# A recurrent mixer with a small expert layer on one core: batch 5's up products move between the last projections, and the up weights' rows are centred

## The reference

```python
shifted = pad(hidden)[:, :-1]
key, value, rec = (hidden * m + shifted * (1 - m) for m in (mix_k, mix_v, mix_r))
k = key @ Wk;  v = value @ Wv;  r = sigmoid(rec @ Wr)
rwkv = _wkv(time_decay, time_first, k, v)     # a recurrence over the 512 tokens
x = layernorm(hidden + (r * rwkv) @ Wo)
...
gate = softmax(x @ router_w.T) * top2_mask     # 8 experts of width 16
h = einsum('bth,eih->beti', x, down_w);  a = silu(h)
out = layernorm(x + sum_e gate_e * (a_e @ up_w_e))
```

## Time and profile before

| | |
|---|---|
| median of 3 runs | 495.65 us (495.41 to 495.65) |
| profiled execution | 495.26 us |
| its span, first to last instruction | 493.4 us |
| TensorE busy | 471.9 us, 96% |
| VectorE busy | 408.8 us, 83% |
| ScalarE busy | 338.7 us, 69% |
| GpSimd busy | 259.5 us, 53% |
| TensorE's granted clock | 0.986 of full speed over the span |

### The profile page before, as it was taken

The page is one execution under the profiler, slowest core; times in us unless marked ns, Lnnn a source line. Parts: engine busy times, 40 slices in busy tenths (PEclk is TensorE's granted clock), DMA queues, the critical chain, the costliest instruction groups (busy, mean ns, idle before and its releaser), DMA issues. The chain is left out here.

```text
span 493.4 us, 6302 instructions
## 1 busy us (share of the span) xinstructions
PE 471.9 (96%) x1850; PEld 316.4 (64%) x1850; DVE 408.8 (83%) x655; ACT 338.7 (69%) x769; POOL 259.5 (53%) x279
## 2 busy tenths in 40 slices
PE   8998799999999999999999999999999999999991
PEld 3444377777777667775777667776677656776550
DVE  6998988897799878997799977998699977776686
ACT  1568365865867678786777769776787767657574
POOL 2446764566515964457625767259635574321326
PEclk9999799999999999999999999999999999999997
DMA  9800250003000042004110032001320012300015
GB/s 248 277 12 1 86 191 1 0 3 85 1 1 0 24 147 87 1 1 129 64 64 1 1 129 106 22 1 63 107 89 1 0 43 86 128 1 1 1 38 219
DMA packets 20098, 30.35 MB, mean 62 GB/s; under 512 B 2016, under 2 KB 7136, under 8 KB 20064
## 3 DMA queue, kind: packets, MB, share of 16 engines
q1 hardware_dynamic: 20064, 29.95, 18.6%
HBM read 21.56 MB, written 8.39 MB: 61 GB/s over the span
## 5 line engine op out<-in xcount | busy, mean ns | idle before, releaser
L514 ACT ACTIVATE PR<-PR 128x512 f32<-128x512 f32 x128 | 74.3, 581 | 53.0 <-PE PR L296 23.1
L320 PE MATMUL PP<-WO,RW 128*128 128x512 f32 x216 | 97.3, 592 | 0.0
L1026 POOL TENSOR_SCALAR NM<-SUM,RS 128x1 f32<-128x1 f32 x30 | 9.1, 302 | 157.3 <-ACT RS L514 157.3
L320 PEld LDWEIGHTS PP<-WO,RW 128*128 128x128 f32 x216 | 39.5, 190 | 41.3 <-issue 40.9
L1020 POOL TENSOR_TENSOR DQ<-DEN,EX 128x512 f32<-128x512 f32 x32 | 41.0, 1282 | 35.4 <-DVE DEN L730 35.4
L767 DVE TENSOR_TENSOR RW<-NU,PR 128x512 f32<-128x512 f32 x32 | 22.0, 687 | 42.3 <-ACT PR L514 42.2
L778 DVE SCALAR_TENSOR_TENSOR KT<-D,VEC,XT 128x512 f32<-128x512 f32 x56 | 52.0, 959 | 0.0
L292 PE MATMUL PV<-VH,WVH 128*128 128x512 f32 x112 | 47.0, 420 | 0.4 <-DVE NU L754 0.4
L292 PE MATMUL PK<-KH,WKH 128*128 128x512 f32 x112 | 47.2, 422 | 0.0
L730 DVE TENSOR_TENSOR_SCAN DEN<-PK,EX 128x512 f32<-128x512 f32 x32 | 39.1, 1221 | 9.7 <-ACT EX L514 7.5
L292 PE MATMUL PR<-RH,WRH 128*128 128x512 f32 x112 | 47.0, 419 | 0.2 <-DVE RW L767 0.2
(11 more groups left out here) (200 smaller groups left out, 1119.2 us busy)
## 6 DMA issues: line engine op xcount, KB each, us to landing
XT<-in_xt SPq DMA_DIRECT2D x32, 256.0 KB, 3.6
XN<-in_x SPq DMA_DIRECT2D x28, 256.0 KB, 2.7
out<-XN SPq DMA_DIRECT2D x28, 256.0 KB, 2.0
WO<-in_wo SPq DMA_DIRECT2D x1, 1024.0 KB, 7.7
XT<-in_x SPq DMA_DIRECT2D x4, 256.0 KB, 4.1
out<-XT SPq DMA_DIRECT2D x4, 256.0 KB, 2.2
X1T<-in_wk SPq DMA_DIRECT2D x2, 256.0 KB, 4.9
XN<-in_wv SPq DMA_DIRECT2D x2, 256.0 KB, 5.3
```

Source lines behind the costliest of these rows:

```text
L320: last = eng.matmul(projected_at(t), RW[(C * b + c) % NRW][:, 128 * n:128 * n + 128], WO[:, c, :], start=(c == 0), stop=(c == C - 1))
L514: eng.activation(*a, **k).then_inc(q[s], 1)
L1026: eng.tensor_scalar(NM1[:, col(t)], total, RS1[:, col(t)], scale, ALU.mult, ALU.mult)\
```

## The change

Three things change, and the queues are rewritten around them.

Order of the up products: in slots 12 to 28 `ffn_up(t3 + 3)` goes behind the projection. In the tail the transposes of batch 6 (`ffn_turn(LAST - 1)`) come ahead of the last projection, into bank PP, and their copy goes to the buffer NU instead of AGT; batch 5's four up products stand between the last projection, the transposes and the hidden products of batch 7.

Centring: the rows of UP (each row belongs to one expert's hidden unit and has 512 outputs) lose their mean once, in slot 4. The tile that the up product is added to is normalised and has mean zero, so the sum has mean zero too. The second norm then needs no mean: the square has no offset, the addition gives no sum, NM falls away, and a normalisation is one multiplication with RS.

Bookkeeping: MEASURED has three tiles (29, 30, 31) instead of five and FINISHED one (31) instead of two; tiles 24 and 25, and 26 and 27, share one logarithm and one exponential (`spread2(t, 2)`).

```diff
-        MEASURED = [NT * (LAST - 2) + 3, NT * (LAST - 1) + 1, NT * (LAST - 1) + 3, NT * LAST + 1, NT * LAST + 3]
+        MEASURED = [NT * LAST + 1, NT * LAST + 2, NT * LAST + 3]
-        FINISHED = [NT * LAST + 1, NT * LAST + 3]
+        FINISHED = [NT * LAST + 3]
...
-                self.agt = (DQ if tail else AGT)[:, 128 * lo:128 * hi]
-                self.turned_at = ((PK[0], PH)[lo // 2] if tail else PK[1] if k == LAST - 1 else PU)[:, 0:128 * (hi - lo)]
+                self.agt = (DQ if tail else NU if k == LAST - 1 else AGT)[:, 128 * lo:128 * hi]
+                self.turned_at = ((PK[0], PH)[lo // 2] if tail else PP if k == LAST - 1 else PU)[:, 0:128 * (hi - lo)]
...
-                if j == 0 and batch(b - 3):
-                    ffn_up(t3 + 3)
                 if j == 0:
                     for t in now[:1]:
                         project(t)
+                if j == 0 and batch(b - 3):
+                    ffn_up(t3 + 3)
...
             turn(t7)
+            ffn_turn(LAST - 1)
+            ffn_up(t5)
             project_most(t7 + 3)
             project_rest(t7 + 3)
             turn(t7 + 1)
             hidden(t7)
+            ffn_up(t5 + 1)
             turn(t7 + 2)
-            ffn_up(t5)
             hidden(t7 + 1)
-            ffn_up(t5 + 1)
+            ffn_up(t5 + 2)
             turn(t7 + 3)
             hidden(t7 + 2)
+            ffn_up(t5 + 3)
             hidden(t7 + 3)
-            ffn_turn(LAST - 1)
-            ffn_up(t5 + 2)
-            ffn_up(t5 + 3)
+            ffn_up(t6)
             ffn_turn(LAST)
-            ffn_up(t6)
...
+            def spread2(t, n=1):
...
+                    for u in range(t, t + n):
+                        eng.wait_ge(q["res2"], u + 1)
+                        act("sq2", JUNK if u == t else KT[0][:, :], xn_at(u), ACT.Square, accum_out=SQ2[:, col(u)])
...
+                if s == C:
+                    eng.wait_ge(q["up"], 16)
+                    act("upx", JUNK, UP[:, :], ACT.Copy, accum_out=SUMU[:, :])
...
             spread(t7 + 2)
+            ffn_out(LAST - 1)
+            spread2(t5)
...
+            ffn_in(LAST)
             turned(t7 + 3)
             hidden_copy(t7 + 2)
-            ffn_in(LAST)
+            spread2(t5 + 1)
             hidden_copy(t7 + 3)
-            ffn_out(LAST - 1)
             ffn_in(LAST + 1)
             ffn_out(LAST)
-            spread2(t5 + 1)
+            spread2(t5 + 2)
             ffn_out(LAST + 1)
-            for t in range(t5 + 2, NT * NB):
+            spread2(t5 + 3)
+            spread2(t6, 2)
+            spread2(t6 + 2, 2)
+            for t in range(t7, NT * NB):
                 spread2(t)
...
             def residual2(t):
                 eng.wait_ge(q["up_"], t + 1)
-                eng.scalar_tensor_tensor(out=xn_at(t), in0=up_at(t), scalar=1.0, in1=xn_at(t), op0=ALU.mult,
-                                         op1=ALU.add, accum_out=SUM2[:, col(t)]).then_inc(q["res2"], 1)
+                eng.tensor_tensor(xn_at(t), up_at(t), xn_at(t), ALU.add).then_inc(q["res2"], 1)
...
             residual(t7 + 2)
+            residual2(t5)
             residual(t7 + 3)
             moments(t7 + 3)
-            residual2(t5)
+            residual2(t5 + 1)
             gate_scores(LAST)
+            residual2(t5 + 2)
             gate_top(LAST)
-            residual2(t5 + 1)
-            residual2(t5 + 2)
+            silu(LAST)
+            residual2(t5 + 3)
             gate_scores(LAST + 1)
-            silu(LAST)
             gate_top(LAST + 1)
-            residual2(t5 + 3)
             silu(LAST + 1)
...
             def normalise2(t):
...
                 eng.wait_ge(q["rs2"], t + 1)
-                eng.tensor_scalar(NM2[:, col(t)], total, RS2[:, col(t)], scale, ALU.mult, ALU.mult)\
-                   .then_inc(q["nm2"], 1)
-                eng.wait_ge(q["nm2"], normalised(t))
-                eng.tensor_scalar(xn_at(t), xn_at(t), RS2[:, col(t)], NM2[:, col(t)], ALU.mult, ALU.add)\
-                   .then_inc(q["nrm2"], 1)
+                eng.tensor_scalar(xn_at(t), xn_at(t), RS2[:, col(t)], None, ALU.mult).then_inc(q["nrm2"], 1)
...
+                if s == C:
+                    eng.wait_ge(q["upx"], 1)
+                    eng.tensor_scalar(NMU[:, :], SUMU[:, :], -1.0 / H, None, ALU.mult).then_inc(q["upm"], 1)
+                    eng.wait_ge(q["upm"], 1)
+                    eng.tensor_scalar(UP[:, :], UP[:, :], NMU[:, :], None, ALU.add).then_inc(q["upc"], 1)
             t5, t6, t7 = (NT * (LAST - i) for i in (2, 1, 0))
-            for n in range(NT):
+            for n in range(NT - 1):
                 normalise(t7 + n)
-            for t in range(t5, NT * NB):
+            normalise2(t5)
+            normalise(t7 + 3)
+            for t in range(t5 + 1, NT * NB):
```

More of the change, by code:

```diff
@@ L74, in rwkv_moe_postln @@
         ST, MV = sb("ST", [128, 7, 6]), sb("MV", [128, 7, 2])
-        SUM2, SQ2, LV2, RS2, NM2 = (sb(n + "2", [128, 3 * NT]) for n in ("SUM", "SQ", "LV", "RS", "NM"))
+        SQ2, LV2, RS2 = (sb(n + "2", [128, 3 * NT]) for n in ("SQ", "LV", "RS"))
+        SUMU, NMU = sb("SUMU", [128, 1]), sb("NMU", [128, 1])
         PK = [bank("PK0"), bank("PK1")]
@@ L377, in hidden @@
                 elif b == LAST and n == 1:
-                    eng.wait_ge(q["res"], NT * LAST + 1)
+                    eng.wait_ge(q["agc"], LAST)
                 elif b == LAST:
@@ L396, in ffn_turn @@
                 elif k == LAST - 1:
-                    eng.wait_ge(q["x1t"], NT * LAST + 3)
+                    eng.wait_ge(q["res"], NT * LAST + 1)
                 elif k == LAST - 2:
@@ L411, in ffn_up @@
                 if t == 0:
-                    eng.wait_ge(q["up"], 16)
+                    eng.wait_ge(q["upc"], 1)
                 eng.wait_ge(q["agc"], k + 1)
@@ L573, in spread @@
                 act("rs1", RS1[:, col(t)], LV1[:, col(t)], ACT.Exp, scale=-0.5)
-            def spread2(t):
+            def spread2(t, n=1):
+                cols = slice(col(t).start, col(t).start + n)
                 if t in MEASURED:
                     i = MEASURED.index(t)
-                    eng.wait_ge(q["mv2"], i + 1)
-                    act("lv2", LV2[:, col(t)], MV[:, i, 1:2], ACT.Ln, bias=EPS)
-                else:
[L581 to L587, removed]
+                    eng.wait_ge(q["mv2"], i + n)
+                    eng.activation(LV2[:, cols], MV[:, i:i + n, 1], ACT.Ln, bias=EPS).then_inc(q["lv2"], n)
+                else:
+                    for u in range(t, t + n):
+                        eng.wait_ge(q["res2"], u + 1)
+                        act("sq2", JUNK if u == t else KT[0][:, :], xn_at(u), ACT.Square, accum_out=SQ2[:, col(u)])
+                    eng.wait_ge(q["sq2"], squared(t + n - 1, MEASURED))
+                    eng.activation(LV2[:, cols], SQ2[:, cols], ACT.Ln, bias=EPS, scale=1.0 / H).then_inc(q["lv2"], n)
+                eng.wait_ge(q["lv2"], t + n)
+                eng.activation(RS2[:, cols], LV2[:, cols], ACT.Exp, scale=-0.5).then_inc(q["rs2"], n)
             def turned(t):
@@ L617, in ffn_out @@
                 eng.wait_ge(q["agt"], k + 1)
-                eng.wait_ge(q["up_"], NT * min(k, LAST - 1))
+                if k < LAST - 1:
+                    eng.wait_ge(q["up_"], NT * k)
+                elif k == LAST - 1:
+                    eng.wait_ge(q["rw"], U)
                 act("agc", p.agt, p.turned_at, ACT.Copy)
@@ L696, in _ @@
             hidden_copy(t7 + 1)
-            spread2(t5)
+            ffn_in(LAST)
             turned(t7 + 3)
             hidden_copy(t7 + 2)
-            ffn_in(LAST)
+            spread2(t5 + 1)
             hidden_copy(t7 + 3)
-            ffn_out(LAST - 1)
             ffn_in(LAST + 1)
             ffn_out(LAST)
-            spread2(t5 + 1)
+            spread2(t5 + 2)
             ffn_out(LAST + 1)
-            for t in range(t5 + 2, NT * NB):
+            spread2(t5 + 3)
+            spread2(t6, 2)
+            spread2(t6 + 2, 2)
+            for t in range(t7, NT * NB):
                 spread2(t)
@@ L808, in finish @@
             def finish(t):
-                i = MEASURED.index(t)
                 eng.wait_ge(q["rs2"], t + 1)
-                eng.tensor_scalar(xn_at(t), xn_at(t), MV[:, i, 0:1], RS2[:, col(t)], ALU.subtract, ALU.mult)\
-                   .then_inc(q["fin"], 1)
+                eng.tensor_scalar(xn_at(t), xn_at(t), RS2[:, col(t)], None, ALU.mult).then_inc(q["fin"], 1)
             def moments2(t):
@@ L969, in _ @@
             residual(t7 + 2)
+            residual2(t5)
             residual(t7 + 3)
             moments(t7 + 3)
-            residual2(t5)
+            residual2(t5 + 1)
             gate_scores(LAST)
+            residual2(t5 + 2)
             gate_top(LAST)
-            residual2(t5 + 1)
-            residual2(t5 + 2)
+            silu(LAST)
+            residual2(t5 + 3)
             gate_scores(LAST + 1)
-            silu(LAST)
             gate_top(LAST + 1)
-            residual2(t5 + 3)
```

(12 more changed lines are left out.)

## The result

The changed kernel takes 497.83 us (median, 497.36 to 498.31) against 495.65 us before: a ratio of 1.0045, 95% interval 1.0027 to 1.0062. It is slower by 2.2 us, where 492.5 with a range of 489.3 to 494.2 was forecast.

The account below looks back on a forecast made before the run. TensorE, busy 96%, and a VectorE-ScalarE ring were taken as bounds, with a shared tail. Loop 5 x (0.70 - 0.53) = 0.85 plus tail 2.23 gave 3.1 us: 495.65 to 492.5 us, range 489.3 to 494.2.

Parts of the forecast that it names:

- Normalisation 2 as one multiplication: GpSimd's second norm: drops 0.26 us and a 0.10 gap per tile, but delays VectorE's second mix 0.53 in five slots.
- the second pair's factor: Tail, ScalarE: factor for the second pair of tiles sharing a logarithm and exponential, forecast ready at 483.6 us.
- third rival: Slower: GpSimd's R subtraction also precedes the second mix, 1.78 late; loop 5.4 worse, 498.8 us; chance 0.05.
- The move: Up product behind the projection, five slots: TensorE 0.87 us ahead each time, ring takes 0.70, 3.5 us in all.
- the ring: VectorE and ScalarE loop of scans, decay gates, receptance, weighing; can gain 0.70 us a batch from an earlier TensorE.
- The room: Before the next slot's decay gates on ScalarE: they could start 0.70 us earlier, at 411.95 instead of 412.65.
- The new wait of TensorE: 0.3 to 0.9 us before the second up product of slots 3 mod 4 or before a receptance product.
- The delay of the mix: VectorE's second mix in slots 11, 15, 19, 23, 27 held by GpSimd's XN: 0.53 us each, bounds 0 and 0.77.
- first rival: The second mix is not delayed: loop gains 3.5 us and tail 2.23, giving 489.9 us; chance 0.20.
- The addition: VectorE's addition loses its sum: priced at 0, with up to 0.08 for each of the last eight, 0.6 us.
- The centring: UP centred once in slot 4 by ScalarE and GpSimd, hidden by TensorE's queue: price 0; 2 us once without cover.
- The tail: After slot 31: GpSimd's last five tiles at 0.77 end at 487.85 instead of 490.08, gaining 2.23 us; bounds 1.1 and 2.9.

Follow-up runs that it names:

- add_zero: Changed kernel with GpSimd's second norm as multiply, then add 0.0, instead of multiply alone; 490.79 us, ratio to before 0.9902.
- move_only: Kernel before with one edit: in slots 12 to 28 the up product goes behind the projection; 493.07 us, ratio 0.9948.
- mult_only: Kernel before with UP centred in slot 4 and GpSimd's second norm as one multiplication, old queues otherwise; 500.86 us, ratio 1.0103.
- old_queues_add_zero: Kernel before with UP centred and GpSimd's second norm as multiply, then add 0.0, in the old queues; 496.96 us, ratio 1.0030.
- order_low: Changed kernel with multiply-add-0.0 norm, tile t2's norm moved between R's second and third low-part subtractions in slots 3 mod 4; 488.84 us, ratio 0.9864.
- forms: Changed kernel with GpSimd's second norm in seven forms in turn by tile number, result still the norm; for durations only, no kernel time given.
- forms2: Changed kernel with seven other forms of GpSimd's second norm, two leaving the tile unscaled; for durations only, no kernel time given.

## Why the prediction was wrong

**The step that failed** is "Normalisation 2 as one multiplication", where each tile "drops a 128x1 operation of 0.26 us and its gap", and with it the tail's "five tiles (26 to 30) at 0.77 each". I took XN's duration over from a form with two operations to one with one operation. It is 1.56. Seven such tiles (24 to 30) stand one behind the other from 481.33, so the five of my sum could not start with the second pair's factor at 483.05 but had to wait for the two ahead of them. At 0.77 a tile those two would have been done by 482.9, and the five would have started 0.09 behind the factor, as in add_zero, and ended at about 487.3 (483.14 + 3.85, and 0.26 by which one of them is longer in add_zero). GpSimd ended at 492.29. By this estimate the price of the form is 5.0 of the 5.3 us; the rest is less than executions differ by in slot 10. The trace before had no row with this form, and I treated it as if it had one: I bounded the delay of the mix from both sides and not the operation itself. None of my rivals had it; the upper end of the range would have needed 1.1 us a tile. The measured time lies near my third rival (498.8), but not for its reason: there the mix was to be 1.78 late behind GpSimd's R subtraction, and it was 0.45 late.

**The move** held. TensorE's five waits are gone and the ring, not TensorE, takes the gain. The room was 0.70 as said, but move_only got 0.47 a batch out of it, since a later mix met GpSimd. The new wait of TensorE that I forecast for slots 3 mod 4 does not show among its waits. It gives its lead back in short gaps instead: in slot 14 of the kernel after, about 0.2 us ahead of a receptance product (201.66) and 0.2 ahead of the transposes (205.17).

**The delay of the mix** held, in its mechanism and nearly in size: 0.45 measured, 0.53 forecast, in each of five batches, and it goes when the place in the queue is given back. The first rival, no delay, fell. The loop of the changed kernel gains 0.93 us, forecast 0.85. That closeness is partly luck. By the scans, a batch lost 0.42 from slot 11 to slot 12 and gained 0.56 from slot 12 to slot 13 (four of the five; 0.71 in the last), where the sum had 0.53 and 0.70: two errors that cancel. The gain is short because the slow XN is still running when the mixes behind the weighing start; in slot 24 the three take 2.22 instead of 2.07. With the quick form they take 2.07, the gain is 0.72 and the loop gains 1.55.

**The addition** without its sum was priced at 0, and that held: the mix follows it by 0.59 (394.69 to 395.28 in slot 27), before by 0.60.

**The centring** cost nothing that shows: mult_only and old_queues_add_zero are level with before in slot 10. The GpSimd addition there took 1.57 and not 0.77, the slow form again, but nothing waited for it.

**The tail** was right in shape. TensorE's 1.02 us wait is gone, a wait of 0.43 ahead of the second half replaced it (0.4 to 0.6 forecast), ScalarE's second pair's factor came at 483.05, or 483.36 on the clock of before, as slot 31 is 0.31 earlier (483.6 forecast). With the quick form the tail is 3.1 shorter where 2.23 was forecast: five tiles at 0.69 and not 0.77 (0.4), the second pair's factor 0.2 sooner, and 0.1 less behind GpSimd's end.

The forecast 492.5 is missed by 5.3 us. With the quick form the same kernel takes 490.79, 1.7 below it: there the loop gives 0.7 and the tail 0.9 more than the sum had.

## What to carry to other kernels

Fewer operations in an instruction is not less time: before an edit changes an instruction's form, time that form, or count its price as unknown, however similar the old one looks. When two engines hold each other up, as VectorE's mixes and GpSimd's norms do here, a small instruction ahead of a large one can decide who goes first; taking it out moves the large one to its place in time, and the cost appears on the other engine. Put such large operations where the other engine waits for something else, as order_low does.

## What the runs showed of the hardware

GpSimd's tensor-scalar on 128x512 float32 takes 0.69 for multiply-add, multiply-multiply and add-multiply with one column and a constant, 0.77 for multiply-add with two columns, 1.57 for one operation alone, and 2.0 to 2.1 for pairs with subtract or maximum and for add-add (runs forms and forms2).

GpSimd held VectorE's second mix for about 0.45 us whether its own operation took 0.69 (add_zero) or 1.56 (after). With the slow form the mix ended at 396.48 + 1.18 = 397.66 and XN at 397.99: a mix needs 0.75, so by this estimate it ran from about 396.9 and the two overlapped for 0.75. With the quick form the mixes end at 394.48 + 2.37 = 396.85 and XN at 396.31, so the overlap is 0.2 at most. The Trainium skill, "SBUF — State Buffer", section "SBUF: two separate sides", says that the one that has the shared pair of ports keeps it for the full instruction. The order that it gives agrees with the trace. The whole length agrees to within 0.2 us for the quick form (add_zero) and does not for the slow one (0.75 of overlap); the profile's spans on GpSimd are rough, so the second is a reading of one kind of record and not a proof.
